# Writing out VectorE's program of the first layer in a two-layer attention and expert kernel

## The reference

```python
x = x + _L0_xattn_ref(_layernorm(x), ctx, ctx, mask_k, ...)   # 16 heads of 8: q from x, k and v from ctx, keys masked
x = x + _L0_ffn_ref(_layernorm(x), w_gate, w1, w2)            # 8 experts, top 2 by logits, softmax gates, relu
x = x + _L1_xattn_ref(_layernorm(x), ctx, mask_q, ...)        # 16 heads of 64, queries masked by -1e6
x = x + _L1_ffn_ref(_layernorm(x), w1, b1, w2, b2)            # dense, 512 wide, relu
```

## Time and profile before

| | us |
|---|---|
| time, median of 3 runs | 938.54 |
| lowest and highest run | 936.5, 940.93 |
| profiled execution, span from first to last instruction | 955.2 |
| first layer up to n = 3 | 0 to 58 |
| first layer, n = 4 to 27 | 58 to 305 |
| first layer, n = 28 and later | 305 to 360 |
| expert stage and start of the second layer | 360 to 590 |
| second layer | 590 to 955 |

### The profile page before, as it was taken

One profiled execution on the slowest core, in us unless ns is written; L12 is line 12 of the kernel. 1 busy time (PEld: TensorE's weight loads), 2 busy tenths in 40 slices (PEclk: granted clock), 3 DMA queues, 4 the chain that ended last, 5 costly groups with the idle time before them and its releaser, 6 DMA issues. The chain is left out here.

```text
span 955.2 us, 29952 instructions
## 1 busy us (share of the span) xinstructions
PE 896.2 (94%) x8399; PEld 785.4 (82%) x8399; DVE 673.3 (70%) x2146; ACT 694.9 (73%) x2694; POOL 446.4 (47%) x739
## 2 busy tenths in 40 slices
PE   5899999999999987999998799999999999999996
PEld 3677766777766777999997699999999999999995
DVE  5788887888888874222222788888787778777873
ACT  2888887888888962333335999998778877887882
POOL 4124433433433453111114777776666666666542
PEclk9999999999999998999999999999999999999998
DMA  5766656666666613222221122222112111211110
GB/s 156 226 212 198 214 186 201 201 204 200 208 214 208 196 41 92 72 71 67 67 92 53 34 62 62 63 68 62 61 45 66 60 59 45 66 60 57 41 51 10
DMA packets 113563, 103.93 MB, mean 109 GB/s; under 512 B 11761, under 2 KB 100627, under 8 KB 113494
## 3 DMA queue, kind: packets, MB, share of 16 engines
q1 hardware_dynamic: 106594, 88.81, 29.8%
q0 software_dynamic: 6112, 13.90, 4.7%
q10 hardware_dynamic: 788, 0.39, 0.1%
HBM read 56.53 MB, written 46.53 MB: 108 GB/s over the span
## 5 line engine op out<-in xcount | busy, mean ns | idle before, releaser
L664 ACT ACTIVATE PR<-PR,nmx 128x128 f32<-128x128 f32 x512 | 198.0, 390 | 8.1 <-DVE nmx L868 5.6
L664 ACT ACTIVATE PR<-bank,nmx 128x128 f32<-128x128 f32 x512 | 182.1, 384 | 6.6 <-issue 6.1
L334 POOL TENSOR_TENSOR PR<-PR,rden 128x512 f32<-128x512 f32 x128 | 133.7, 1044 | 92.2 <-DVE rden L873 85.8
L1149 PE MATMUL bank<-ident,PR 128*128 128x128 f32 x1024 | 156.7, 276 | 4.5 <-POOL PR L334 1.6
L1149 PEld LDWEIGHTS bank<-ident,PR 128*128 128x128 f32 x1024 | 118.8, 141 | 49.5 <-issue 40.8
L664 ACT ACTIVATION_READ_ACCUMULATOR PR<-bank,nmx 128x1 f32 x512 | 114.6, 224 | 0.0
L758 ACT ACTIVATE H<-bank 128x512 f32<-128x512 f32 x70 | 41.8, 597 | 90.4 <-PE bank L1355 90.4
L1383 PE MATMUL bank<-XCT,wqk 128*128 128x128 f32 x832 | 103.7, 278 | 0.7 <-ACT XCT L652 0.7
L1383 PEld LDWEIGHTS bank<-XCT,wqk 128*128 128x128 f32 x832 | 96.9, 192 | 3.5 <-ACT XCT L652 1.0
L664 ACT ACTIVATION_READ_ACCUMULATOR PR<-PR,nmx 128x1 f32 x512 | 96.8, 189 | 0.0
L868 DVE TENSOR_REDUCE nmx<-bank 128x4 f32<-128x512 f32 x128 | 86.6, 676 | 12.8 <-PE bank L1189 12.1
(11 more groups left out here) (196 smaller groups left out, 2092.2 us busy)
## 6 DMA issues: line engine op xcount, KB each, us to landing
second_layer_values<-wide SPq DMA_DIRECT2D x32, 512.0 KB, 3.0
wide<-second_layer_values SPq DMA_DIRECT2D x32, 512.0 KB
expert_outputs<-HF SPq DMA_DIRECT2D x32, 256.0 KB
expert_outputs<-HF SPq DMA_DIRECT2D x64, 128.0 KB, 1.9
KBD<-expert_outputs SPq DMA_DIRECT2D x128, 64.0 KB
QS<-expert_outputs SPq DMA_DIRECT2D x32, 256.0 KB
PR<-expert_inputs SPq DMA_DIRECT2D x36, 128.0 KB, 2.0
expert_outputs<-PR POOLq DMA_DIRECT2D x35, 128.0 KB, 2.0
```

What stands on the lines that cost most here:

```text
L334: nc.gpsimd.tensor_tensor(unit, unit, rden[:, p, G * g:G * g + G].unsqueeze(2).broadcast_to([P, G, P]), ALU.mult).then_inc(s["nm"], 1)
L664: last = nc.scalar.activation(PR[:, g, j * P:(j + 1) * P], scored, ACT.Exp, bias=nmx[:, p, h:h + 1], accum_out=den[:, p, h:h + 1])
L1149: last = nc.tensor.transpose(T_BANK[g % 2][:, j * P:(j + 1) * P], PR[:, g, j * P:(j + 1) * P], ident[:])
```

## The change

VectorE's first layer is no longer given to `over_steps` but to a new function, `straight_steps`, which calls the step function with an integer n for all steps from -3 to 35. It calls `late_inputs` at the same n as before (4, 10, 16, 22, 28). Waits and addresses of the 24 former loop steps are then constants, with no register operation and no branch. The order of operations stays. `wait_apart` no longer waits for `const_ready` where all counts are integers; this holds for every engine, in steps that are written out (n up to 3 and from 28 on in the first layer, and the written-out steps of the second). The four other engines keep their loops, and VectorE keeps its loops in the expert stage and the second layer.

```diff
@@ -78,6 +78,16 @@
     if between:
         between(len(cuts) - 1)
     for n in range(2 * loop_end, last + 1):
+        step(n, n % 2)
+
+
+def straight_steps(step, first, last, ahead, behind, between=None, every=3):
+
+    loop_start, loop_end = (behind + 1) // 2, (NB - 1 - ahead) // 2
+    cuts = {2 * c: k for k, c in enumerate(list(range(loop_start, loop_end, every)) + [loop_end])}
+    for n in range(first, last + 1):
+        if between and n in cuts:
+            between(cuts[n])
         step(n, n % 2)
 
 
@@ -256,7 +266,8 @@
         def wait_apart(engine, *counts):
 
             counts = [(s, v if isinstance(v, int) else engine.to_reg(v)) for s, v in counts]
-            engine.wait_ge(const_ready, 1)
+            if not all(isinstance(v, int) for _, v in counts):
+                engine.wait_ge(const_ready, 1)
             for s, v in counts:
                 wait(engine, s, v)
 
@@ -971,7 +982,7 @@
                     dve.wait_ge(a["rts"], n)
                     wait(dve, a["o"], n - 2)
                     nc.vector.tensor_tensor(OT0[:, q, :], O_BANK, RTS[:], ALU.mult).then_inc(a["oN"], 1)
-            over_steps(dve, step0, -3, NB + 3, 3, 4, late_inputs)
+            straight_steps(step0, -3, NB + 3, 3, 4, late_inputs)
```

## The result

| | before | after |
|---|---|---|
| time, median | 938.67 (4 runs, 936.5 to 940.93) | 925.54 (4 runs, 923.89 to 928.22) |
| profiled execution: span | 955.2 | 921.6 (time 923.89) |

The ratio is 0.9865, 95% interval 0.9837 to 0.9892: 13.1 us less, more than twice the 5.0 predicted and outside the range of 930.0 to 939.5. So kernels are compared within one batch, and "the 938 level" and "the 959 level" name the two.

The account below looks back on a forecast made before the run. The prediction took TensorE to bound the first layer's loop steps, delayed by VectorE at loop ends. Terms -7.0, +1.2 and +0.75 sum to -5.05, taken as -5.0: 938.54 to 933.5 us, range 930.0 to 939.5.

Parts of the forecast that it names:

- part A: VectorE's loop ends in the first layer go; ten long steps become short ones: 7.0 us off.
- Part B: VectorE's longer written-out program: three more crossings into new code at 0.4 us, +1.2 us (bounds 0 and +6.9).
- Part C: QS loads for TensorE, nearly late already, give back part of the gain: 0.25 and 0.5, together +0.75 us.
- Small edits: Dropped const_ready waits in head and tail steps lie behind other waits: 0; if none were covered, -0.6 us.
- Rival 3: Crossings into new program are free: 6.25 or 7.1 us off, 931.4 us; chance 0.12.
- Rival 1: Late L906 only hides other lateness; only sequencer operations at loop ends are saved: 1.2 us, 937.3; chance 0.19.
- Rival 2: QS bounds the stage's last third, from 243 us on; only seven long steps count: 3.45 us off, 935.1; chance 0.12.
- rival 4: Program fetches on VectorE arrive late: five crossings cost 24 us, 956 us, slower; chance 0.07.

Follow-up runs that it names:

- before_look: The kernel before, unchanged, run again for a profile beside its timed runs: 938.97 us, span 936.2.
- after_again: The changed kernel, unchanged, run again beside the kernel before on one chip: 926.13 us, ratio 0.9875 to the kernel before.
- straight_keep: The changed kernel with the wait for const_ready kept everywhere, in a batch where the kernel before took 959.1 us: 956.21 us, ratio 0.9967.
- keep_spread: The changed kernel with const_ready waits kept and the loads of out_bias and fb moved from k = 2 to k = 3: 952.5 us, ratio 0.9934.
- three_step_pairs: The kernel before with three pairs of steps in VectorE's loop body, 4 loop ends where 12 were, registers kept: 948.29 us, ratio 1.0098.
- straight_keep_again: The changed kernel with const_ready waits kept, run again in a batch where the changed kernel took 926.13 us: 930.22 us, ratio 0.9907.

## Why the prediction was wrong

**The step that failed** stands in part A: "The register operations inside a step, also removed, save nothing more: short steps have them too and TensorE is busy for 9.62 of their 9.86 us." The steps' own waits and register operations are nearly the whole gain: 12.5 us in the 25 steps, of about 13, and little or none of it at the loops' ends. On VectorE they cost 0.36 us a step in idle time and 0.24 by pushing the cast into the scatter. The argument had two faults.

First, a busy TensorE was read as TensorE at work. The same 79 or 80 matmuls are busy for 9.37 to 9.55 us in before_look and for 9.03 to 9.08 in after_again: a step's true need is about 9.05, and the rest was pace set by VectorE, hidden in matmuls whose ends are modelled. The last head step before the loops, written out already, took 9.08 us in the first profile too (L973 at 48.95 and 58.03), though without scatters, with 30 of 35 VectorE instructions and without the two smallest matmuls. The prediction passed it over.

Second, "a difference of microseconds carries over" from the profile of 955.2 to the median of 938.54. It doesn't: the profile was of the 959 level, where TensorE's late signals are in the step and VectorE's savings vanish in them. There the written-out kernel gains 3.2 us (straight_keep), or 6.3 with the three loads moved (keep_spread). A forecast of 5.0 was near that in size, but by luck: the steps became 9.9 to 10.2 us long, not the 9.85 of the short ones. The 16.7 us between span and median was the warning; the prediction blamed tracing.

**Part A's own 7.0 us.** A long step isn't long by its loop's end: in three_step_pairs they alternate without one. The late L888 and L906 of the earlier trace rows belong to the 959 level, where L973 still waits when the branch comes; in before_look the branch is done before, and L888 comes 0.20 us behind L973 in every step. What removing the ends alone gives at the 938 level is about nothing; the difference of long and short is inside the step too.

**Part B** (+1.2): nothing. (A loop body holds some 132 instructions of VectorE and its sequencer by the trace, where the prediction reckoned with 105 or more.) The changed kernel has one unreleased idle time of 0.2 us in 242; before_look had five, 1.5 us together. The rule of the Trainium skill cited there ("Runtime: NRT & Kernel Launch", Instruction fetch mechanics: crossing a boundary is mostly hidden) holds for code in a line. The same section's other rule, that a taken branch outside the fetched window stalls, fits rows that there now are: 2.6 and 2.7 us in three_step_pairs. That a fetch is what VectorE stood for there isn't shown.

**Part C** (+0.75): TensorE waits for QS 2.4 us in two places, 0.5 us more than the earlier trace rows. A pair at one level, before_look and after_again, shows 1.96 and 1.90 us at the main one. About 0 to 0.5.

**Small edits** (0): true of ordinary steps. Whether the waits on const_ready have a part in the late QS that makes up half of the 4.1 us between straight_keep_again and after_again is open.

**The rivals.** Rival 3 (crossings are free) was right on its point. Rival 1 was right that taking the late L906 away isn't what gives the time, and wrong on what follows (1.2 us in all). Rival 2 didn't come; rival 4 came only where a body of six steps jumped back. None of them had VectorE's whole step as the bound, which is what it was.

## What to carry to other kernels

Before a profile carries a sum, compare its span with the timed runs; if they differ by more than the runs scatter, find out in what before pricing anything. A busy share of 95% doesn't say that an engine bounds a stage: take the same instructions where nothing disturbs them, and see what they need. Writing out a loop whose steps hold many waits and addresses from registers can save a third of a microsecond a step on the engine that runs them, and more where a short saving moves an instruction out of a collision with GpSimd.

## What the runs showed of the hardware

- A cast of 128x2 on VectorE that starts more than 0.60 us into GpSimd's DMA_INDIRECT of 1.10 us ends with it (up to 0.47 us, for 0.16); started earlier it isn't held (484 casts, with the exceptions named above).
- In some batches, for all kernels of the batch, TensorE's signals behind its values matmuls come late and bunched (0.09 us apart for 0.44), after GpSimd's second scatter has ended; written-out steps are some 1.0 us longer than in others (straight_keep against straight_keep_again), and the kernel before takes 959 us for 938.6. One chip showed both in different batches. Its cause stays open, and the changed kernel itself was never run at that level.
- A jump back over six steps (some 370 instructions) costs VectorE 2.6 to 2.7 us; over two steps, nothing that rows show.
